# A radial product laid on 128 partitions, and two products with y merged into one instruction

## What is computed

```python
w1 = rbf @ W_rbf                                    # layer 0: edge weights, E x 224
m1_s, m1_v = _cg_tp(msg_s, msg_v, y0, y1, w1[:, :CS], w1[:, CS:2 * CS], ...)
...
w = edge_query @ tp_weight                          # layer 1
out2 = 2.0 ** (-0.5) * (w2a * sh_s)[:, :, None] * ev + 0.5 * w2b[:, :, None] * jnp.cross(ev, sh_v[:, None, :])
out3 = 3.0 ** (-0.5) * w3 * jnp.sum(ev * sh_v[:, None, :], axis=-1)
...
agg = jax.ops.segment_sum(edge_x, edge_dst, num_segments=n)
```

## Time and profile before

| | us |
|---|---|
| median of three runs | 7991.2 |
| the three runs | 7987.54, 7991.20, 7993.15 |
| the profiled execution | 7987.12 |
| its span | 7985.3 |
| VectorE busy | 7640.4 (96%) |
| TensorE busy | 7044.2 (88%) |
| ScalarE, GpSimd busy | 5259.3 and 5304.9 (66% each) |

### The profile page before, as it was taken

The page is one execution under the profiler, slowest core; times in us unless marked ns, Lnnn a source line. Parts: engine busy times, 40 slices in busy tenths (PEclk is TensorE's granted clock), DMA queues, the critical chain, the costliest instruction groups (busy, mean ns, idle before and its releaser), DMA issues. The chain is left out here.

```text
span 7985.3 us, 199893 instructions
## 1 busy us (share of the span) xinstructions
PE 7044.2 (88%) x48227; PEld 5904.8 (74%) x48227; DVE 7640.4 (96%) x19067; ACT 5259.3 (66%) x18286; POOL 5304.9 (66%) x5500
## 2 busy tenths in 40 slices
PE   6899999999999999999999859998888888888888
PEld 4888888888888888888888848875555555555556
DVE  5999999999999999999999889976999999999999
ACT  2666666666666666666666634435777777777775
POOL 2777777777777777777777426634777777777772
PEclk5999999999999999999999979977999999999999
DMA  3444344433443333443333337732333333333332
GB/s 104 107 109 105 105 106 105 106 105 104 106 105 106 105 105 106 105 106 105 105 106 106 84 130 261 258 115 69 93 89 90 89 89 88 89 89 89 90 89 58
DMA packets 789804, 854.44 MB, mean 107 GB/s; under 512 B 413920, under 2 KB 571488, under 8 KB 789216
## 3 DMA queue, kind: packets, MB, share of 16 engines
q0 software_dynamic: 241920, 413.20, 21.2%
q1 hardware_dynamic: 547232, 436.34, 18.3%
q10 hardware_dynamic: 576, 4.01, 0.1%
HBM read 704.54 MB, written 148.44 MB: 107 GB/s over the span
## 5 line engine op out<-in xcount | busy, mean ns | idle before, releaser
L1242 POOL DMA_INDIRECT agg<-tab_conv,ce_idx x1808 | 1708.7, 945 | 866.5 <-issue 616.0
L468 POOL DMA_INDIRECT ae_gsrc<-tab_src,ae_idx x1616 | 1533.5, 949 | 751.3 <-issue 446.9
L471 POOL DMA_INDIRECT ae_gdst<-tab_dst,ae_idx x1616 | 1645.9, 1019 | 539.6 <-issue 539.6
L1331 PE MATMUL psum<-ce_prod,ce_plain 128*128 128x384 f32 x3616 | 1539.7, 508 | 328.5 <-DVE ce_prod L1304 275.7
L1316 ACT ACTIVATE ce_prod<-ce_raw,ce_y 128x64 f32<-128x64 f32 x5424 | 1463.8, 332 | 0.0
L1314 ACT ACTIVATE ce_prod<-ce_raw,ce_y 128x160 f32<-128x160 f32 x1808 | 752.2, 416 | 514.5 <-DVE ce_raw L1263 514.5
L713 ACT ACTIVATE ae_second_t<-psum 128x512 f32<-128x512 f32 x1212 | 732.1, 604 | 507.3 <-PE psum L623 500.1
L1333 PEld LDWEIGHTS psum<-ce_prod,ce_plain 128*128 128x128 f32 x3616 | 687.7, 190 | 479.5 <-issue 1.5
L1331 PEld LDWEIGHTS psum<-ce_prod,ce_plain 128*128 128x128 f32 x3616 | 546.9, 191 | 475.4 <-DVE ce_plain L1292 345.5
L631 PE MATMUL psum<-pack_sb,ae_first_t 128*128 128x200 f32 x3232 | 850.1, 345 | 2.2 <-ACT ae_first_t L709 2.0
L641 PE MATMUL psum<-pack_sb,ae_second_t 128*128 128x96 f32 x3232 | 664.4, 287 | 129.1 <-ACT ae_second_t L713 126.6
(11 more groups left out here) (217 smaller groups left out, 18692.7 us busy)
## 6 DMA issues: line engine op xcount, KB each, us to landing
ag_val<-h_dram SPq DMA_DIRECT2D x452, 320.0 KB, 4.1
h_dram<-ae_hout SPq DMA_DIRECT2D x404, 320.0 KB
agg<-in_query SPq DMA_DIRECT2D x452, 128.0 KB
ae_rin<-in_rin SPq DMA_DIRECT2D x404, 128.0 KB
agg<-tab_conv,ce_idx POOLq DMA_INDIRECT x1808
ae_gsrc<-tab_src,ae_idx POOLq DMA_INDIRECT x1616
ae_gdst<-tab_dst,ae_idx POOLq DMA_INDIRECT x1616
ce_idx<-in_eidx SPq DMA_DIRECT2D x452, 4.0 KB
```

Source lines behind the costliest of these rows:

```text
L468: pool.indirect_dma_start(gsrc[t.slot4][:, k, :], None, g["tab_src"], bass.IndirectOffsetOnAxis(ap=idx[t.slot4][:, k:k + 1], axis=0))\
L471: pool.indirect_dma_start(gdst[t.slot4][:, k, :], None, g["tab_dst"], bass.IndirectOffsetOnAxis(ap=idx[t.slot4][:, 4 + k:5 + k], axis=0))\
L1242: pool.indirect_dma_start(node[t.slot8][:, k, :], None, g["tab_conv"], bass.IndirectOffsetOnAxis(ap=idx[t.slot8][:, k:k + 1], axis=0))\
L1331: pe.matmul(b_a[t.slot], plain[t.slot4][:, k, :], prod[t.slot][:, k, 96:480], start=(k == 0), stop=False, skip_group_check=True)
```

## The change

In attention `rin` and `rbfy` are laid out anew: each of the four edges k has its own 32 partitions, so the product has 128 partitions and 128 elements. A matmul's row group is now 64 partitions, that hold two edges k. So that each gets its own result, `wy` is 448 columns wide: in its first half the rows of the other edge (32 to 63, 96 to 127) are zero, in its second half those of the first. In the convolution `diag` and `plus` are parts of one tensor `both`, and one instruction of 768 elements writes both. For this y is stored as eight numbers (y0, y1, y2, y3, y2, y3, y1, y2) in place of six, and the copy `yp` takes seven of them. `minus` stays in PSUM with its own instruction.

```diff
-    ("iota", 128, 128), ("wy", 64, WY), ("m1_0", 128, 200), ("m1_1", 128, 96), ("m1_2", 96, 96), ("val_t", 64, 128),
+    ("iota", 128, 128), ("wy", 128, 2 * WY), ("m1_0", 128, 200), ("m1_1", 128, 96), ("m1_2", 96, 96), ("val_t", 64, 128),
...
-        rin = [sb(f"rin{u}", [64, 512]) for u in range(4)]
-        rbfy = [sb(f"rbfy{u}", [64, 256]) for u in range(2)]
+        rin = [sb(f"rin{u}", [P, 2 * P]) for u in range(4)]
+        rbfy = [sb(f"rbfy{u}", [P, P]) for u in range(2)]
...
-                        dve.tensor_tensor(rbfy[t.slot][:, :], rin[t.slot4][:, 0:256], rin[t.slot4][:, 256:512], ALU.mult)\
+                        dve.tensor_tensor(rbfy[t.slot][:, :], rin[t.slot4][:, 0:P], rin[t.slot4][:, P:2 * P], ALU.mult)\
                             .then_inc(spread, 1)
...
                         for k in (0, 2, 1, 3):
-                            q, e = 32 * (k // 2), P * (k % 2)
-                            ins = pe.matmul(b_w[:, k, :], rbfy[t.slot][q:q + 32, e:e + P], w("wy")[q:q + 32, :], start=True, stop=True)
+                            q, half = slice(64 * (k // 2), 64 * (k // 2) + 64), WY * (k % 2)
+                            ins = pe.matmul(b_w[:, k, :], rbfy[t.slot][q, :], w("wy")[q, half:half + WY], start=True, stop=True)
...
-        y_ring = sb("y", [P, 8, 4, 6])
+        y_ring = sb("y", [P, 8, 4, 8])
...
-        diag, plus = sb("diag", [P, 4, 3, CV]), sb("plus", [P, 4, 3, CV])
+        both = sb("both", [P, 4, 2, 3, CV])
+        diag, plus = both[:, :, 0, :, :], both[:, :, 1, :, :]
...
-        yp = [banks[6][:, 384 + 24 * u:408 + 24 * u].rearrange("p (k j) -> p k j", k=4) for u in range(2)]
+        yp = [banks[6][:, 384 + 28 * u:412 + 28 * u].rearrange("p (k j) -> p k j", k=4) for u in range(2)]
...
-                        for d, out in enumerate((diag[:, :, :, :], plus[:, :, :, :], minus)):
-                            ins = dve.tensor_tensor(out, comps(here[:, :, CS:C]),
-                                                    yp[t.slot][:, :, 1 + d:4 + d].unsqueeze(3).to_broadcast(three), ALU.mult)
-                        ins.then_inc(outer_done, 1)
+                        dve.tensor_tensor(both[:, :, :, :, :].rearrange("p k d x c -> p k d (x c)"),
+                                          here[:, :, CS:C].unsqueeze(2).to_broadcast([P, 4, 2, V3]),
+                                          yp[t.slot][:, :, 0:6].unsqueeze(3).to_broadcast([P, 4, 6, CV]), ALU.mult)
+                        dve.tensor_tensor(minus, comps(here[:, :, CS:C]), yp[t.slot][:, :, 4:7].unsqueeze(3).to_broadcast(three),
+                                          ALU.mult).then_inc(outer_done, 1)
...
-                        dve.tensor_copy(yp[t.slot], y[t.slot8][:, :, :]).then_inc(turned_y, 1)
+                        dve.tensor_copy(yp[t.slot], y[t.slot8][:, :, 1:8]).then_inc(turned_y, 1)
...
-    for lo in (0, 32):
-        W["wy"][lo:lo + 16, 0:64], W["wy"][lo:lo + 16, 192:224] = ss, vs
-        W["wy"][lo + 16:lo + 32, 64:128], W["wy"][lo + 16:lo + 32, 128:160], W["wy"][lo + 16:lo + 32, 160:192] = sv, vv0, vv1
+    for lo in (0, 32, 64, 96):
+        own = W["wy"][lo:lo + 32, WY * (lo // 32 % 2):]
+        own[0:16, 0:64], own[0:16, 192:224] = ss, vs
+        own[16:32, 64:128], own[16:32, 128:160], own[16:32, 160:192] = sv, vv0, vv1
```

More of the change, by code:

```diff
@@ L1535, in lay_inputs @@
     ey6 = y.reshape(SUPER, 4, P, 4)[..., [0, 1, 2, 3, 1, 2]].transpose(0, 2, 1, 3).reshape(SUPER, P, 24)
[L1537 to L1540 removed]
+    ey8 = y.reshape(SUPER, 4, P, 4)[..., [0, 1, 2, 3, 2, 3, 1, 2]].transpose(0, 2, 1, 3).reshape(SUPER, P, 32)
+    rbf = np.pad(np.asarray(i["edge_attr_16"]), ((0, E - EDGES), (0, 0))).reshape(SUPER, 4, P, 16).transpose(0, 1, 3, 2)
+    y0 = np.broadcast_to(y[:, :, 0].reshape(SUPER, 4, 1, P), rbf.shape)
+    left = np.concatenate([rbf, rbf], 2).reshape(SUPER, P, P)
+    right = np.concatenate([y0, np.ones_like(rbf)], 2).reshape(SUPER, P, P)
     query = np.pad(np.asarray(i["edge_attr_64"]), ((0, E - EDGES), (0, 0))).reshape(SUPER, 2, 256, 64)
@@ L1543, in lay_inputs @@
     return dict(
-        pack=lay_pack(i), x=x, eidx=eidx, ey6=ey6, sdst=sdst, dst3=dst3,
+        pack=lay_pack(i), x=x, eidx=eidx, ey6=ey6, ey8=ey8, sdst=sdst, dst3=dst3,
         rin=np.concatenate([left, right], 2), yall=y.reshape(4 * SUPER, P, 4).transpose(1, 0, 2),
```

6 lines of the change are left out of this document (1 added, 5 removed).

## The result

| | before | after |
|---|---|---|
| median, us (four runs each) | 7992.17 | 7920.11 |
| lowest to highest | 7987.54 to 7994.04 | 7914.60 to 7924.55 |
| the profiled execution, its span | 7987.12, 7985.3 | 7914.60, 7912.8 |

The ratio is 0.9912, with a 95% interval of 0.9899 to 0.9924: 72 us or 0.9% faster, 10 us from the forecast of 7910 and inside its range. Where a kernel had slow executions beside fast ones, a ratio here compares the fast ones alone, so that for e9 to e11 it is not the quotient of two medians. Between the two profiled spans lie 72.5 us. First the page of the kernel after: totals, VectorE's tenths and the granted clock in 40 slices (beside the earlier trace rows), queue q1 (beside the earlier trace rows).

What follows compares the result with a forecast made beforehand. VectorE's queue was taken to bound both long loops. From the profiled 7987.1 us, 53 us (attention) and 27 us (convolution) go, leaving 7907; the median 4 us above gives 7911, forecast 7910, range 7890 to 7940.

Steps and rivals of the forecast that it cites:

- The bound: In both long loops, the length of a step is VectorE's queue: 10.84 us in attention, 5.36 us in the convolution.
- E: Rival: products cost by elements on all partitions together, and the wide one runs as two; 7991 us, chance 0.01.
- L521, 64x256 to 128x128: Attention's radial product on VectorE falls from 0.33 to 0.20 us; 404 x 0.13 = 53 us saved, bounds 48 to 57.
- The matmuls and the load: Attention's 64-row matmuls (L681) and the load of rin in 128 rows: cost 0 for each.
- The other bound: Attention's matmul row groups no longer run beside each other: eight passes take 1.7 us, +0.65 us a step.
- A: Rival: 64-row matmuls lose their pairing, TensorE's step becomes 10.8 us, attention gains nothing; 7963 us, chance 0.05.
- The merge: Convolution, diag and plus in one instruction: 0.063 us less 0.004 for y's copy, x 452 = 27 us, bounds 20 to 31.
- Rival C: Merging in the convolution returns the whole fixed part of the duration, 0.134 us a step; 7878 us, chance 0.03.
- Who is late next: In the convolution ScalarE's end releases TensorE's sum, at no cost; slack ahead of L1260 shrinks from 0.35 to some 0.24 us.
- The clock (D): Rival: TensorE's granted clock drops in a long stage; twenty steps 8.9 us longer give 8088 us, chance 0.03.
- The median: Whole kernel: profiled execution forecast at 7907 us, plus 4 us by which the median lies above it, gives 7911 us.

Runs made afterwards that it cites:

- e9: e8 with e6's convolution (three products in one instruction); ratio 0.9814, median 11721.3 us on chips with stops, where the kernel before takes 12,035 us.
- e11: The changed kernel once more, unaltered, on chips with stops where the kernel before takes 12,035 us; median 11819.0 us, ratio 0.9933.
- e3: Changed kernel, with GpSimd's attention gathers also waiting for the end of VectorE's L599; 7915.84 us, ratio 0.9906.
- e4: Changed kernel, with the four radial matmuls in order 0, 1, 2, 3, so both of one row group follow each other; 7915.29 us, ratio 0.9904.
- e5: Changed kernel, with each radial matmul contracting over all 128 rows, three quarters of the weights zero; 7917.57 us, ratio 0.9911.
- e2: Kernel before, with the convolution part of the change only; 7964.46 us, ratio 0.9965.
- e6: Changed kernel, with all three convolution products in one instruction of 1152 elements, minus in SBUF, y as ten numbers; 7894.64 us, ratio 0.988.
- e8: e7 plus diag and plus of attention's first product group merged into one 768-element product; 7862.73 us, ratio 0.9843.
- e7: Changed kernel, without attention's copy of y into PSUM at L564, so product L586 reads y from SBUF; 7889.86 us, ratio 0.9875.
- e1: Kernel before, with the attention part of the change only; 7942.72 us, ratio 0.994.

## Why the prediction was right, and where it was off

- **The bound.** Right: VectorE's queue is a step in both loops, and distances between starts carried over to new shapes. Durations would have misled, in the convolution above all, where they grew while the step shrank. E has nothing for it: L521 is 0.20 us from the reduce, and VectorE shows one 768-wide product.
- **L521, 64x256 to 128x128.** 0.13 us forecast, 0.131 measured. The term of the sum was still too large, 53 us for 46, below its bound of 48: it took every neighbour's time as fixed. 0.017 us a step came back, 0.010 at L570, where the shorter step put GpSimd's gathers into the costly moments of its start (table above, e3), and 0.007 at L553, for which no cause is shown. I had asked whether GpSimd would become late, and not whether its new place beside VectorE would cost something. That the loss stayed so small is luck: the same encounter costs up to 0.075 us in a step.
- **The matmuls and the load.** Cost 0, right for the matmuls by e4 and e5. The load had no run of its own; L521 shows no idle time in front of it. The other bound was sized well for the passes (+0.65 forecast, 0.64 measured from the first pass to the next group) and wrong in price: e5 ran that case and lost nothing, as A's step of 10.8 us came out at 10.71. Only 0.02 us a step of the wait was left there, so even that case was cleared narrowly.
- **The merge.** 27 us forecast, 26 to 28 measured (after, e2). It returned 0.064 us in the convolution, 0.065 in e6's second merge (0.465 + 0.862 - 1.262, means), and 0.064 in e8. Rival C, with 0.134, did not come. Nor did the 0.125 us estimated from the Trainium skill's PSUM row (VectorE: DVE Perf Modes, section "The TRN2 errata"): the measured 0.06 us stay with its SBUF row, in all three merges.
- **Who is late next.** ScalarE releases the sum, as forecast, and it costs nothing; the slack is 0.21 us for 0.24 in the mean. What is missing goes with the longer completions of VectorE, on which ScalarE's start depends: at the start of the stage (5500 to 5600 us), where L1306 lasts 0.30 us in the mean, the slack is 0.27, and from 6900 us on, at 0.37 us, it is 0.20.
- **The clock (D).** The clock row is the same as before in all 40 slices, full in both long stages.
- **The median.** 7911 by the sum, 7920 measured: 7 us from attention, 1 from the convolution, and 1.4 as the median lies 5.5 us above the profiled execution and not 4. The narrow range, 7898 to 7922, leaves these 4 us out at its lower end; with them the bounds of the terms give 7903 to 7923.

## What to carry to other kernels

Where one engine is always busy, cost an edit by the distance from start to start, and merge instructions that share their inputs: here each merge is worth 0.06 us, from 384 to 768 elements and from 768 to 1152. Do the same for the engine that you fear: e5's passes were 0.73 us longer by duration and took 0.53 us of TensorE's wait, and that decided it.

Before removing work from the busy engine, look at what the others do at the same moment. A GpSimd gather and a VectorE product with both inputs in SBUF meet, and 0.05 us of shift decide which of them pays. But don't take an engine without waits for one at its limit: compare its instructions with their shortest form. GpSimd in e8 has no wait, and 0.6 us of its step are holds. Here leaving out a copy into PSUM (e7) gained 28 to 30 us though it let a product meet the gathers.

## What was not expected of the hardware

- **The encounter of GpSimd and VectorE** also lengthens VectorE's side, by up to 0.08 us (0.90 for 0.82), when the gather starts between 0.04 us ahead of L570 and 0.045 us behind its start; the later in that stretch, the more. Beyond it the gather is held (0.95 up to 1.6 us), and ahead of it neither pays.
- **Passes over 64 rows or fewer** follow each other in 0.10 us for 224 columns, those over 128 rows in 0.20 (1.03 and 1.75 us for eight), also within one row group.
- **Two engines in step.** In e7 and e8 the faster engine is held at the same two products in every step, and neither shows a wait for the other.
- **Durations that drift.** In the convolution of every kernel with the 768-wide product on an undisturbed chip (after, e2 to e5, e7, e8) all VectorE instructions grow longer together, though not steadily (e7 ends at 0.28 again), while their starts stay as far apart. L1306 in the kernel after, at the start and at the end of the stage:

```profile
5441.76 0.28 DVE L1306 TENSOR_TENSOR ce_prod<-psum,ce_dot 128x128 f32<-128x128 f32 x1
5502.09 0.31 DVE L1306 TENSOR_TENSOR ce_prod<-psum,ce_dot 128x128 f32<-128x128 f32 x1
...
7826.99 0.41 DVE L1306 TENSOR_TENSOR ce_prod<-psum,ce_dot 128x128 f32<-128x128 f32 x1
```

It is real: ScalarE, which waits for the end of L1264, starts 0.68 us after its start over 6000 to 7600 us, and 0.59 us in the kernel before (L1263), 0.05 us after the end in both. The kernels without that product (before, e1) and the one with 1152 elements (e6) hold their durations to 0.02 us. The form alone does not do it: e8 has a 768-wide product in attention as well (L497), and there it lasts 0.935 to 0.953 us through the stage; and e11 never exceeds 0.31 us for L1306. In both VectorE pauses again and again, for L559's wait or at the stops; whether that is the reason was not tried. The cause stays open; it cost nothing here, since the slack ahead of L1261 took it up.
